# Adding seven expert groups' rows through a DRAM table, and expert weights in long runs, in a two-layer attention and mixture-of-experts kernel

## The chip, the cores and the metric

The kernel runs on one core of a Trainium2 chip. The metric is device time in microseconds (us), lower is better. Times shown are the median of three runs and, for the trace, one profiled execution.

## What is computed

Four sequences of 256 tokens with 256 features (1024 tokens) go through two layers. The change touches only the end of the second one, the expert part:

```python
probs = jax.nn.softmax(x @ Wr, axis=-1)                       # 32 experts
topw, topi = jax.lax.top_k(probs, K)                          # K = 4 per token
topw = topw / jnp.sum(topw, axis=-1, keepdims=True)
shared = silu(x @ Wsg) * (x @ Wsu) @ Wsd                      # shared expert
shared = shared * jax.nn.sigmoid(x @ Wse)
xe = jnp.zeros((E, CAP, h), x.dtype).at[sel, posc].add(x[tok] * valid[:, None])   # CAP = 32 slots
g = silu(jnp.einsum('ech,ehf->ecf', xe, Wg))
u = jnp.einsum('ech,ehf->ecf', xe, Wu)
ye = jnp.einsum('ecf,efh->ech', g * u, Wd)
y_pair = ye[sel, posc] * (w * valid)[:, None]
out = shared.at[tok].add(y_pair)
```

Beside it stands the second attention, whose values are weighed, transposed and multiplied by a projection. The output is the first layer's x plus that projection, the shared expert and the experts' weighted rows.

## The kernel before

Bass code with a block for each engine; each block is a list of instructions in a fixed order, tied to the others by semaphores. Arrays of tokens are eight tiles of 128 tokens by 256 features.

**Experts.** 32 experts times 32 slots are 1024 slots, handled as `GR` = 8 groups of 128 slots (four experts each). For each group GpSimd (POOL) gathers the rows of its tokens from the DRAM table `token_rows` (line 624), and the list `EXPERT_STEPS` (lines 33 to 43) sets the order in which every engine takes its part. For TensorE (PE): "slots" transposes the gathered rows, "up" (line 1317) multiplies by Wg and Wu, "turn" transposes the hidden rows, "down" (line 1337) multiplies by Wd into bank 7, "sd" (lines 1350 and 1352) is a tile of the shared expert's second product. In the first four tiles of "sd" both operands are plain float32; in the others, and in the projection, each operand is split into a rounded high and a low part, and `mm3` (lines 945 to 947) adds three products.

**Mixing.** After "down" VectorE (DVE) copies a group's output to `YE` (line 1889), ScalarE (ACT) writes its weighted high part `YH` (line 891), DVE the low part `YL` (line 1859). DVE also builds for each group a mask `GT[g]` of 128 slots by 1024 tokens (line 1855). For every one of the eight token tiles PE then multiplies each group's mask by `YH` and by `YL` (lines 1361 and 1362: 2 x 8 x 8 = 128 products) and adds the projection's six into the same bank. "mix" steps bring the first six groups of four tiles forward into the list; the rest comes behind it.

**Second attention's values.** POOL multiplies probabilities by values and adds them (lines 634 and 638, 32 instructions for eight tiles), PE transposes the result (line 1400), ACT and DVE split it, `mix_proj` multiplies.

**Loads.** SyncE (SP) issues nearly all DMAs (lines 482 to 508): for each group two of Wg and Wu (704 KB each, runs of 176 floats) and two of Wd, into four places that are used twice. Groups 4 to 7 wait until the place is free.

**End.** DVE adds each finished bank into `X` (line 1870), SP stores the tile (line 511).

Of the kernel before, what the change touches and what calls it, by code (L numbers as in the profile page):

```python
# [34 lines left out]
                 ("turn", 0), ("slots", 3), ("up", 2), ("down", 0), ("turn", 1), ("slots", 4), ("up", 3), ("down", 1), ("turn", 2), ("sd", 1),  # L35
                 ("mask", (4, 5)), ("split", 0), ("weigh", 0), ("down", 2), ("turn", 3), ("split", 1), ("split", 2), ("sd", 2),
                 ("split", 3), ("down", 3),
                 ("up", 4), ("slots", 5), ("split", 4), ("sd", 3), ("split", 5), ("turn", 4), ("split", 6), ("up", 5), ("slots", 6),
                 ("mask", (6,)), ("down", 4), ("mask", (0,)), ("sd", 4), ("mask", (1, 2)), ("turn", 5),
                 ("mask", (3,)), ("sd", 5), ("mask", (7,)), ("down", 5),  # L40
                 ("high", 0), ("up", 6), ("slots", 7), ("high", 3), ("low", 0), ("sd", 6), ("turn", 6), ("low", 3),
                 ("sd", 7), ("add", 7), ("down", 6), ("mix", 0), ("mix", 1), ("up", 7), ("mix", 2), ("turn", 7),
                 ("mix", 3), ("down", 7)]
# [14 lines left out]
TC = 2 * E1 + 1  # L58
EPS = 1e-5
MASKED = -1.0e30  # L60


def program(nc, a, out):
    ctx = ExitStack()
    with ctx:
# [113 lines left out]
        WD = [w.rearrange("p (e c n) -> p e c n", e=EPG, c=2)  # L179
# [3 lines left out]
        def up_weights(g, e):  # L183
# [5 lines left out]
        GT = [nc.alloc_sbuf_tensor_at(f"GT{g}", [P, N], FR, offset=at)  # L189
              for g, at in enumerate([at0 + 4 * N * k for k in range(4)] + [at0 + 4 * (28672 + N * k) for k in range(2)]  # L190
                                     + [at_xt + 4 * (5 * C * N // 2), at1 + 4 * 2944])]
        YH = nc.alloc_sbuf_tensor_at("YH", [P, GR, D], FR, offset=at0 + 4 * GR * N)
        YL = OS[:, 1].rearrange("p s h n -> p (s h n)").rearrange("p (g n) -> p g n", g=GR)
        TK = IT = FRF[:, 2944:2944 + N]
        HTE = region(15872, 512).rearrange("p (i k n) -> p i k n", i=2, k=2)
# [50 lines left out]
        s_x = [sem(f"x_loaded{b}") for b in range(B)]  # L246
# [1710 lines left out]
```

## Time and profile before

| | |
|---|---|
| median of 3 runs | 428.7 us (428.68 to 429.19) |
| the profiled execution's own time | 429.21 us |
| its span in the trace | 426.8 us |
| granted TensorE clock | 1.0 of full speed |
| PE, PEld busy | 98%, 88% |
| DVE, ACT, POOL busy | 73%, 58%, 40% |
| DMA traffic | 34.45 MB, mean 81 GB/s |

The span is the time from the first to the last recorded event; the execution's own time is 2.4 us longer. PE is the multiplying part of TensorE, PEld its loading of weights, which runs beside it. A matmul's recorded duration contains its way through the array, so that neighbours overlap: what one costs in a row of many is the distance from start to start. A plain float32 product is recorded as two instructions. Times in the trace count from the start of the span.

### The profile page before, as it was taken

The numbers are of one execution on the slowest core, as the hardware profiler recorded it, in microseconds if no ns is written. First come the engines' busy times: TensorE is split into PE (matmuls) and PEld (weight loads), VectorE is DVE, ScalarE is ACT, GpSimd is POOL, SyncE is SP. The second block draws the span as 40 slices with busy tenths as digits, with TensorE's granted clock in tenths as the row PEclk, the third lists the DMA queues.
The fourth block names the chain that finished last, engine by engine and source line by source line (L and its number), as shares of the span: only waits on it lengthen the run. The fifth ranks groups of instructions, "written<-read, shape, count | busy, mean of one in ns | idle before, by whom it ended". The sixth has DMA issues, their size and how long they took to land.

```text
span 426.8 us, 8853 instructions
## 1 busy us (share of the span) xinstructions
PE 419.8 (98%) x3070; PEld 377.2 (88%) x3070; DVE 310.9 (73%) x910; ACT 247.5 (58%) x671; POOL 168.6 (40%) x293
## 2 busy tenths in 40 slices
PE   8999999999999999999999999999999999999997
PEld 8788879999999999999999999999997777567797
DVE  5967575787787888787877767657689994688442
ACT  4666741887868788777867786434314622563120
POOL 3520002645554554554554530102077007699200
DMA  7800020501010101010000000000099942899002
GB/s 214 303 2 1 2 76 25 198 1 51 2 51 0 51 2 51 2 52 1 2 0 3 2 2 0 27 14 12 26 321 300 307 115 88 236 305 279 9 14 86
DMA packets 37754, 34.45 MB, mean 81 GB/s; under 512 B 2448, under 2 KB 35920, under 8 KB 37712
## 3 DMA queue, kind: packets, MB, share of 16 engines
q1 hardware_dynamic: 37328, 32.85, 26.2%
q0 software_dynamic: 384, 1.05, 0.8%
q8 instruction: 25, 0.41, 0.4%
q14 instruction: 17, 0.14, 0.1%
HBM read 31.80 MB, written 2.10 MB: 79 GB/s over the span
## 4 chain that ended last, share of the span: by engine, by line
PE 92%; DVE 5%; ACT 2%; issue 1%; POOL 0%; POOLq 0%; DVEq 0%
PE bank L945 21%; PE bank L947 21%; PE bank L946 21%; PE bank L1116 5%; PE bank L1128 3%; PE bank L1107 3%; PE bank L1350 2%; PE bank L1317 2%; PE bank L1361 2%; PE bank L1362 2%; PE bank L1158 2%; PE bank L1337 2%; DVE OS L1859 1%; PE bank L1022 1%; PE bank L1266 1%; DVE arena L1499 1%
## 5 line engine op out<-in xcount | busy, mean ns | idle before, releaser
L587 POOL TENSOR_TENSOR arena<-arena,rinv 128x384 f32<-128x384 f32 x64 | 52.9, 828 | 81.0 <-DVE rinv L1629 81.0
L945 PE MATMUL bank<-XTl,WA 128*128 128x512 f32 (+1 forms) x126 | 52.0, 412 | 0.9 <-DVE arena L1499 0.8
L947 PE MATMUL bank<-XTh,WA 128*128 128x512 f32 (+1 forms) x126 | 49.1, 390 | 0.0
L946 PE MATMUL bank<-XTh,WA 128*128 128x512 f32 (+1 forms) x126 | 49.1, 389 | 0.0
L771 ACT ACTIVATE PT<-bank 128x256 fp32r<-128x256 f32 x64 | 24.5, 383 | 34.0 <-PE bank L1116 34.0
L1633 DVE TENSOR_TENSOR PT<-bank,PT 128x256 fp32r<-128x256 f32 x64 | 27.2, 425 | 18.8 <-ACT arena L772 18.8
L945 PE MATMUL bank<-WA,XTh 128*128 128x256 f32 x128 | 38.3, 299 | 0.0
L578 POOL CAST Q<-arena 128x128 fp32r<-128x128 f32 x64 | 18.7, 292 | 47.0 <-PE bank L947 47.0
L946 PE MATMUL bank<-WA,XTl 128*128 128x256 f32 x128 | 35.7, 279 | 0.0
L947 PE MATMUL bank<-WA,XTh 128*128 128x256 f32 x128 | 35.7, 279 | 0.0
L1621 DVE CUSTOM_DVE_ANT_0 arena<-bank,posm 128x128 f32<-128x128 f32 x64 | 18.1, 283 | 20.8 <-PE bank L947 20.8
L764 ACT ACTIVATE arena<-arena,nmax 128x256 f32<-128x256 f32 x64 | 32.3, 505 | 0.0
L580 POOL TENSOR_TENSOR Q<-arena,Q 128x128 fp32r<-128x128 f32 x64 | 29.6, 463 | 5.1
L1116 PE MATMUL bank<-ident,arena 128*128 128x128 f32 x192 | 31.4, 272 | 0.0
L777 ACT ACTIVATE arena<-bank,VC 128x256 f32<-128x256 f32 x64 | 30.1, 470 | 0.1
L945 PEld LDWEIGHTS bank<-XTl,WA 128*128 128x128 f32 x126 | 23.8, 189 | 5.5 <-issue 1.7
L947 PEld LDWEIGHTS bank<-XTh,WA 128*128 128x128 f32 x126 | 23.7, 188 | 5.3
L680 ACT ACTIVATE arena<-bank,bqs 128x512 f32<-128x512 f32 x16 | 18.4, 1148 | 15.6 <-PE bank L947 14.7
L946 PEld LDWEIGHTS bank<-XTh,WA 128*128 128x128 f32 x126 | 23.8, 189 | 3.8
L1623 DVE CUSTOM_DVE_ANT_0 arena<-bank,posm 128x256 f32<-128x256 f32 x64 | 26.8, 419 | 0.0
L762 ACT ACTIVATE arena<-arena,nmax 128x128 f32<-128x128 f32 x64 | 25.9, 404 | 1.6 <-DVE nmax L1623 1.1
L749 ACT ACTIVATE K<-bank,VC 128x512 fp32r<-128x512 f32 x32 | 22.0, 688 | 7.5 <-PE bank L947 7.5
(329 smaller groups left out, 1455.5 us busy)
## 6 DMA issues: line engine op xcount, KB each, us to landing
arena<-in_L_ffn_Wg SPq DMA_DIRECT2D x6, 704.0 KB, 7.8
arena<-in_L_ffn_Wu SPq DMA_DIRECT2D x6, 704.0 KB, 10.3
arena<-in_L_ffn_Wd SPq DMA_DIRECT2D x6, 512.0 KB, 7.2
arena<-in_L_attn_Wk SPq DMA_DIRECT2D x8, 256.0 KB, 2.6
arena<-in_L_attn_Wv SPq DMA_DIRECT2D x8, 256.0 KB, 3.2
arena<-in_L_attn_Wo SPq DMA_DIRECT2D x1, 2048.0 KB, 8.4
arena<-in_L_ffn_Wd SPq DMA_DIRECT2D x6, 192.0 KB, 7.6
arena<-in_L_attn_Wq SPq DMA_DIRECT2D x4, 256.0 KB, 4.7
```

The lines of the kernel that those rows point to most:

```text
L580: pool.tensor_tensor(QL[:, u % 3], q, QH[:, u % 3].bitcast(F32), ALU.subtract).then_inc(s_qh, 1)
L587: pool.tensor_tensor(pr, pr, r[:, :, None].to_broadcast([P, 3, P]), ALU.mult).then_inc(s_p, 1)
L762: nc.scalar.activation(Pb[i][:, 0:128], Pb[i][:, 0:128], ACT.Exp, bias=nmax[:, i, 0:1], scale=-1.0, accum_out=psumr[:, i, 0:1])
L764: nc.scalar.activation(Pb[i][:, 128:384], Pb[i][:, 128:384], ACT.Exp, bias=nmax[:, i, 1:2], scale=-1.0, accum_out=psumr[:, i, 1:2]).then_i ...
L771: nc.scalar.activation(PTH[:, u % 2], pb[2 + u % 2][:, 0:256], ACT.Copy)
L777: nc.scalar.activation(QO[:, h, b], pb[4 + u % 2][:, 0:256], ACT.Identity, bias=VC[:, 32 + h:33 + h]).then_inc(s_Oc, 1)
L945: pe.matmul(dst, wh, xl, start=start, stop=False)
L946: pe.matmul(dst, wl, xh, start=False, stop=False)
L947: return pe.matmul(dst, wh, xh, start=False, stop=stop)
L1116: ins = pe.transpose(pb[2 + u % 2][:, P * i:P * i + P], Pb[u % 3][:, P * i:P * i + P], ident[:])
L1623: nc.vector.tensor_tensor_reduce(Pb[i][:, 128:384], bank[:, 128:384], MASK, -1.0, -MASKED, ALU.add, ALU.min, nmax[:, i, 1:2]).then_inc(s_m, 1)
L1633: nc.vector.tensor_tensor(PTL[:, u % 2], pb[2 + u % 2][:, 0:256], PTH[:, u % 2].bitcast(F32), ALU.subtract).then_inc(s_Tl, 1)
```

## The change

**Experts' rows.** Groups 0 to 6 no longer go through masks. ACT writes a group's weighted output, in float32, to `YW` (`y_weighted`). PE multiplies it by a 128 x 128 matrix `SAME[:, g]`, which is 1 where two slots of the group belong to one token ("merge", `expert_merge`), so that each of those slots holds the sum for its token. ACT copies the sum to `YZ` (`y_merged`), and POOL adds the 128 rows into a DRAM table `expert_rows` by an indirect DMA that accumulates (`scatter`), one behind the other: each waits until the one before has landed. Slots whose token came earlier in the group are sent to a spare row. SP fills the table with zeros near the start of the kernel, and at the end, after the seventh scatter has landed, loads it back in four DMAs of 256 KB; DVE adds it to `X` (`add_rows`). Group 7 still uses a mask, one pair of products for each tile.

**What this needs.** Two products of one row by 512 columns (in `table_turn`) spread the slots' token numbers; DVE compares them (`same_token`), POOL clears the part above the diagonal (`BEFORE`), DVE forms the list of rows (`row_places`).

**Order.** `EXPERT_STEPS` has "merge", "ranks", "values" and "ao" steps in place of "high", "low", "mix" and most "mask" steps. "ao" brings the transposes of the values forward. The last tile's values move from POOL to DVE (`last_values`, 7 instructions), POOL follows the list `PV_STEPS`. "sd" alternates between two banks in place of three.

**Weights.** numpy lays out Wg and Wu side by side and ordered by partition, Wd likewise; a group's "up" weights are one DMA (two where its place has two parts) with 11264 bytes in a run for each partition, and Wd's runs are 4096 bytes.

```diff
-                 ("sd", 7), ("add", 7), ("down", 6), ("mix", 0), ("mix", 1), ("up", 7), ("mix", 2), ("turn", 7),
-                 ("mix", 3), ("down", 7)]
...
+                 ("down", 5), ("values", 0), ("turn", 6), ("sd", 5), ("merge", 5), ("down", 6), ("up", 7), ("values", 1), ("merge", 6), ("sd", 6),
+                 ("turn", 7), ("ao", 0), ("down", 7), ("ao", 1), ("sd", 7), ("add", 7)]
...
+LAST = GR - 1
...
+FINAL_BANK = (1, 4, 5, 6, 0, 2, 7, 3)
+PV_STEPS = [("values", 0, 0, 1), ("values", 1, 0, 1), ("values", 2, 0, 2), ("scatter", 0), ("values", 3, 0, 2), ("scatter", 1),
+            ("values", 4, 0, 3), ("scatter", 2), ("values", 5, 0, 3), ("scatter", 3), ("values", 6, 0, 2), ("scatter", 4),
+            ("values", 6, 2, 4), ("scatter", 5), ("scatter", 6)]
...
-            return (0, 2, 3)[j % 3]
+            return (0, 2)[j % 2]
...
+            sp.dma_start(expert_rows.rearrange("(g p) d -> p g d", p=P), ZR[:, None, :].to_broadcast([P, GR + 1, D])).then_inc(s_xs, 16)
...
+                m = EPG // len(WGU[i])
+                for h, part in enumerate(up_parts[i]):
+                    sp.dma_start(part, a["experts_up"][g, :, m * h:m * h + m].rearrange("p e c n -> p (e c n)")).then_inc(s_ew[i], 16)
...
+            sp.wait_ge(s_xg[LAST - 1], 32)
+            for k in range(B):
+                sp.dma_start(YS[:, 2 * k:2 * k + 2], expert_rows[2 * P * k:2 * P * k + 2 * P].rearrange("(g p) d -> p g d", p=P)).then_inc(s_x[k], 16)
...
+            pool.wait_ge(s_gt, 2)
+            pool.affine_select(out=BEFORE, in_=SAME[:, 0:LAST], compare_op=ALU.is_gt, fill=0.0, base=0,
+                               pattern=[[0, LAST], [-1, P]], channel_multiplier=1).then_inc(s_it, 1)
+            pool.iota(IT, [[1, N]], base=1, channel_multiplier=0, allow_small_or_imprecise_dtypes=True).then_inc(s_it, 1)
...
+            def scatter(g):
+                if g == 0:
+                    pool.wait_ge(s_rk, 1)
+                else:
+                    pool.wait_ge(s_xg[g - 1], 32)
+                pool.wait_ge(s_yr, g + 1)
+                pool.indirect_dma_start(expert_rows, bass.IndirectOffsetOnAxis(ap=rank[:, g:g + 1], axis=0), YZ[:, g % 2], None,
+                                        compute_op=ALU.add).then_inc(s_xg[g], 16)
...
+            def y_weighted(g):
+                act.wait_ge(s_dn, g + 1)
+                act.wait_ge(s_sw1, 1)
+                if g == LAST:
+                    nc.scalar.activation(YH[:], pb[7][:, 0:D], ACT.Copy, scale=slot_w[:, g:g + 1]).then_inc(s_ye, 1)
+                    return
+                if g >= 2:
+                    act.wait_ge(s_mg, g - 1)
+                nc.scalar.activation(YW[:, g % 2], pb[7][:, 0:D], ACT.Copy, scale=slot_w[:, g:g + 1]).then_inc(s_ye, 1)
+
+            def y_merged(g):
+                act.wait_ge(s_mg, g + 1)
+                if g >= 2:
+                    act.wait_ge(s_xg[g - 2], 32)
+                nc.scalar.activation(YZ[:, g % 2], pb[3][:, 0:D], ACT.Copy).then_inc(s_yr, 1)
...
+                for half in range(2):
+                    ins = pe.matmul(pb[4 + half][:], onesr[0:1, :], TKr[0:1, 512 * half:512 * half + 512], start=True, stop=True)
+                    ins.then_inc(s_tt, 1)
...
+            def expert_merge(g):
+                pe.wait_ge(s_ye, g + 1)
+                if g >= 1:
+                    pe.wait_ge(s_yr, g)
+                pe.matmul(pb[3][:, 0:D], SAME[:, g], YW[:, g % 2], start=True, stop=True).then_inc(s_mg, 1)
...
-            def mix_groups(j, groups, start, stop):
-                dst, ts = mix_tile(j)
-                for g in groups:
-                    pe.matmul(dst, GT[g][:, ts], YH[:, g], start=start and g == groups[0], stop=False)
-                    ins = pe.matmul(dst, GT[g][:, ts], YL[:, g], start=False, stop=stop and g == groups[-1])
-                return ins
...
+            def values_turn(half):
+                if half == 0:
                     pe.wait_ge(s_xe, GR)
-                    pe.wait_ge(s_gt, GR)
-                    pe.wait_ge(s_yl, 6)
-                mix_groups(j, range(6), True, False)
+                    pe.wait_ge(s_eh, GR - 1)
+                    pe.wait_ge(s_pv, 8)
+                else:
+                    pe.wait_ge(s_eh, GR)
+                    pe.wait_ge(s_ec, GR)
+                    pe.wait_ge(s_pv, 25)
+                    pe.wait_ge(s_pd, 1)
+                for c in range(C):
+                    for i in range(4):
+                        ins = pe.transpose(pb[ao_bank(c, half)][:, P * i:P * i + P], AO[:, 4 * half + i, P * c:P * c + P], ident[:])
+                    ins.then_inc(s_at, 1)
...
+            def final_tile(j):
+                dst, ts = pb[FINAL_BANK[j]][:, 0:D], slice(P * j, P * j + P)
                 for c in range(C):
-                    ins = mm3(dst, AOTh[:, c, ts], AOTl[:, c, ts], PJh[:, c], PJl[:, c], False, c == C - 1)
-                ins.then_inc(s_fo, 1)
-
-            for j in range(4):
-                mix_groups(j, range(6, GR), False, False)
-            for j in range(4, NT):
-                pe.wait_ge(s_al, j - 3)
-                mix_groups(j, range(GR), True, False)
+                    mm3(dst, AOTh[:, c, ts], AOTl[:, c, ts], PJh[:, c], PJl[:, c], c == 0, False)
+                pe.matmul(dst, GT[:, ts], YH[:], start=False, stop=False)
+                pe.matmul(dst, GT[:, ts], YL[:], start=False, stop=True).then_inc(s_fo, 1)
+
+            pe.wait_ge(s_pjl, 1)
+            pe.wait_ge(s_al, 4)
+            pe.wait_ge(s_gt, 3)
+            pe.wait_ge(s_ye, GR + 1)
+            for j in range(NT):
                 if j == 4:
-                    pe.wait_ge(s_al, 4)
-                    pe.wait_ge(s_pjl, 1)
-                mix_proj(j - 4)
-            for j in range(4, NT):
-                mix_proj(j)
+                    pe.wait_ge(s_x2, NT - 1)
+                if j == 5:
+                    pe.wait_ge(s_x2, NT)
+                if j == NT - 1:
+                    pe.wait_ge(s_yr, LAST)
+                final_tile(j)
...
+            def same_token(half):
+                n = 4 if half == 0 else LAST - 4
+                dve.wait_ge(s_tt, 2 + half)
+                nc.vector.scalar_tensor_tensor(out=SAME[:, 4 * half:4 * half + n], in0=pb[4 + half][:, 0:P * n].rearrange("p (g n) -> p g n", g=n),
+                                               scalar=1.0, in1=slot_t[:, 4 * half:4 * half + n, None].to_broadcast([P, n, P]),
+                                               op0=ALU.max, op1=ALU.is_equal).then_inc(s_gt, 1)
+
+            def row_places():
+                dve.wait_ge(s_it, 4)
+                nc.vector.tensor_reduce(earlier[:], BEFORE, AX, ALU.add)
+                step(nc.vector.tensor_scalar(slot_d[:], slot_t[:, 0:LAST], spare[:, 0:1], None, ALU.subtract))
+                step(nc.vector.scalar_tensor_tensor(out=slot_d[:], in0=earlier[:], scalar=0.0, in1=slot_d[:], op0=ALU.is_gt, op1=ALU.mult))
+                nc.vector.scalar_tensor_tensor(out=rank[:], in0=slot_t[:, 0:LAST], scalar=-1.0, in1=slot_d[:],
+                                               op0=ALU.add, op1=ALU.subtract).then_inc(s_rk, 1)
+
+            def last_values(part):
+                j = NT - 1
+                for k in (0, 1) if part == 0 else (2, 3):
+                    dst = AO[:, j] if k == 0 else pvt2
+                    p, v = value_operands(j, k)
+                    step(nc.vector.tensor_tensor(dst.rearrange("p (g r d) -> p g r d", g=G1, r=4), p, v, ALU.mult))
+                    if k:
+                        ins = nc.vector.tensor_tensor(AO[:, j], AO[:, j], pvt2, ALU.add)
+                        if k == 3:
+                            ins.then_inc(s_pd, 1)
+                        else:
+                            step(ins)
+
+            def last_low():
+                dve.wait_ge(s_ye, GR)
+                nc.vector.scalar_tensor_tensor(out=YL[:], in0=pb[7][:, 0:D], scalar=slot_w[:, LAST:GR], in1=YH[:].bitcast(F32),
+                                               op0=ALU.mult, op1=ALU.subtract).then_inc(s_ye, 1)
+
+            def add_rows(j):
+                dve.wait_ge(s_x[j // 2], 32)
+                step(nc.vector.tensor_tensor(X[:, j], YS[:, j], X[:, j], ALU.add))
...
+    up = np.concatenate([given['L1_ffn_Wg'], given['L1_ffn_Wu']], axis=2)
+    out['experts_up'] = up.reshape(GR, EPG, C, P, 2 * F1).transpose(0, 3, 1, 2, 4)
+    out['experts_down'] = given['L1_ffn_Wd'].reshape(GR, EPG, F1, D).transpose(0, 2, 1, 3).reshape(GR, F1, EPG * D)
```

The last part of the PE program, before: down of group 7 (L1337), all transposes of the values (L1400), then masks times `YH` and `YL` (in `OS`); 56 more such pairs and the 48 products of the projection follow or stand between.

```order
L1337 MATMUL bank<-WAF,arena 32x256 x8
L1400 MATMUL bank<-ident,arena 128x128 x16
L1361 MATMUL bank<-YH,GT_73 128x256
L1362 MATMUL bank<-OS,GT_73 128x256
L1361 MATMUL bank<-YH,GT_74 128x256
L1362 MATMUL bank<-OS,GT_74 128x256
```

Now (rows of three kinds: L1397 is down, L1377 up, L1405 merge, L1387 and L1388 turn, L1433 transposes of the values; between the merge and the turn stand the 18 products of sd 6, before the last rows the 18 of sd 7):

```order
L1397 MATMUL bank<-arena 32x256 x8
L1377 MATMUL bank<-arena 32x352 x8
L1405 MATMUL bank<-YX,arena 128x256
...
L1387 MATMUL bank<-ident,arena 128x128
L1388 MATMUL bank<-ident,arena 48x128
L1433 MATMUL bank<-ident,arena 128x128 x8
L1397 MATMUL bank<-WAF,arena 32x256 x8
L1433 MATMUL bank<-ident,arena 128x128 x8
...
L1464 MATMUL bank<-Y_69,GT 128x256
L1465 MATMUL bank<-Y_70,GT 128x256
```

A tile's end is now the projection's six products and one pair for group 7; the sums of groups 0 to 6 have left the PE program but for one merge each.

POOL behind the gathers, before (L634 multiplies, L638 adds; the end of its program):

```order
L634 TENSOR_TENSOR pvt<-arena 128x256
L638 TENSOR_TENSOR arena<-arena,pvt 128x256
L634 TENSOR_TENSOR pvt<-arena 128x256
L638 TENSOR_TENSOR arena<-arena,pvt 128x256
L65 UNCONDITIONAL_BRANCH
```

And now (L665 and L669 are the same two, L679 a scatter):

```order
L679 DMA expert_rows<-YX_68,rank 1152x256
L665 TENSOR_TENSOR pvt<-arena 128x256
L669 TENSOR_TENSOR arena<-arena,pvt 128x256
L665 TENSOR_TENSOR pvt<-arena 128x256
L669 TENSOR_TENSOR arena<-arena,pvt 128x256
L679 DMA expert_rows<-YX_68,rank 1152x256 x2
L68 UNCONDITIONAL_BRANCH
```

The scatters stand among the values; between the fifth and the sixth are four value instructions, between the sixth and the seventh none.

## Rows read from the trace of the kernel before

**Rows 1.** The chain that ended last, by engine (the page).
```profile
PE 92%; DVE 5%; ACT 2%; issue 1%; POOL 0%; POOLq 0%; DVEq 0%
```
**Rows 2.** Stretches: us, busy time (and instructions) of each engine, clock, DMA share, GB/s.
```profile
365.00:385.00 20.00, 20.00 (x198) 12.23 (x196) 15.72 (x28) 12.14 (x29) 16.93 (x19) 1.00 1.13 298
385.00:398.00 13.00, 13.00 (x134) 10.56 (x126) 11.85 (x20) 3.96 (x12) 11.31 (x14) 1.00 0.84 211
398.00:407.00 9.00, 8.60 (x86) 6.89 (x82) 1.06 (x4) 1.26 (x4) 0.00 (x0) 1.00 0.01 2
407.00:427.00 20.00, 17.15 (x148) 16.85 (x144) 7.78 (x16) 2.98 (x6) 0.00 (x0) 1.00 0.15 53
```
**Rows 3.** PE's waits from 350 us: us in total, times, longest.
```profile
PE bank L1361 <- DVE X L1864: 0.4, 1, 0.4
```
**Rows 4.** PE groups by line from 350 us: count | busy us, mean ns | idle before.
```profile
L1361 PE MATMUL bank<-YH,GT 128*128 128x256 f32 x64 | 15.9, 288 | 0.4 <-DVE X L1864 0.4
L1362 PE MATMUL bank<-OS,GT 128*128 128x256 f32 x64 | 15.5, 281 | 0.0
```
**Rows 5.** PE and DVE in order of time: start, us, what.
```profile
340.82 0.63 PE L1266 MATMUL bank<-FRX,TW 128*65 128x512 f32 x2
341.29 0.40 PE L945 MATMUL bank<-XTl,OS 128*128 128x512 f32 x1
...
370.60 1.46 PE L1350 MATMUL bank<-FRF,arena 128*128 128x256 f32 x6
371.90 1.03 PE L1350 MATMUL bank<-FRF,WAF 128*128 128x256 f32 x4
372.76 0.59 PE L1350 MATMUL bank<-FRF,arena 128*128 128x256 f32 x2
373.29 1.07 PE L1337 MATMUL bank<-arena 128*32 128x256 f32 x16
...
410.07 0.28 PE L1361 MATMUL bank<-YH,GT 128*128 128x256 f32 x1
...
411.01 0.28 PE L1361 MATMUL bank<-YH,GT 128*128 128x256 f32 x1
...
424.26 0.42 DVE L1870 TENSOR_TENSOR X<-bank,X 128x256 f32<-128x256 f32 x1 [0.28 <-PE bank L947]
```
**Rows 6.** ACT groups by line from 350 us.
```profile
L891 ACT ACTIVATE YH<-arena,slot_w 128x256 fp32r<-128x256 f32 x8 | 3.6, 502 | 8.6 <-DVE arena L1889 5.8 <-PE bank L1337 2.7
L903 ACT ACTIVATE arena<-bank 128x256 f32<-128x256 f32 x8 | 3.0, 380 | 0.1
```
**Rows 7.** POOL in order of time.
```profile
353.92 0.95 POOL L624 DMA_INDIRECT arena<-token_rows,idx  x1 [0.30 <-issue]
...
366.66 2.09 POOL L634 TENSOR_TENSOR arena<-arena 128x256 f32<-128x256 f32 x3 [3.27 <-DVE arena L1793]
...
391.74 0.65 POOL L634 TENSOR_TENSOR arena<-arena 128x256 f32<-128x256 f32 x1
```
**Rows 8.** DMA issues: count, KB each, us from issue to landing.
```profile
arena<-in_L_attn_Wk SPq DMA_DIRECT2D x8, 256.0 KB, 2.6
arena<-token_rows,idx POOLq DMA_INDIRECT x8, 2.8
out<-X SPq DMA_DIRECT2D x8, 128.0 KB, 1.7
arena<-in_L_ffn_Wu SPq DMA_DIRECT2D x3, 704.0 KB, 10.1
```
**Rows 9.** The stores of `token_rows`, from issue to landing.
```profile
DMA to landing us min/median/max: 1.7/1.7/8.0
```
**Rows 10.** SP's last issue of Wu, and PE's first product that reads it.
```profile
383.88 2.01 SPq L495 DMA_DIRECT2D arena<-in_L_ffn_Wu  x1
...
401.50 1.39 PE L1317 MATMUL bank<-arena 128*32 128x352 f32 x16
```
**Rows 11.** DVE groups by line from 350 us.
```profile
L1855 DVE TENSOR_SCALAR GT<-FRF,slot_t 128x1024 fp32r<-128x1024 f32 x8 | 7.7, 991 | 0.0
L1859 DVE SCALAR_TENSOR_TENSOR OS<-arena,slot_w,YH 128x256 fp32r<-128x256 f32 x8 | 5.4, 708 | 0.2 <-ACT YH L891 0.2
L1870 DVE TENSOR_TENSOR X<-bank,X 128x256 f32<-128x256 f32 x8 | 3.4, 425 | 9.4 <-PE bank L947 9.4
L1889 DVE COPY arena<-bank 128x256 f32<-128x256 f32 x8 | 3.3, 418 | 4.0 <-PE bank L1337 3.9
```

More of the change, by code:

```diff
@@ L243, in program @@
         pvt = sb("pvt", [P, 256])
-        s_x = [sem(f"x_loaded{b}") for b in range(B)]
+        onesr = sb("onesr", [1, P], FR)
+        spare = sb("spare", [P, 1])
+        earlier = sb("earlier", [P, LAST])
+        slot_d = sb("slot_d", [P, LAST])
+        rank = sb("rank", [P, LAST], U32)
+        expert_rows = nc.dram_tensor("expert_rows", (N + P, D), F32, kind="Internal").ap()
+        s_x = [sem(f"x_then_expert_rows_loaded{b}") for b in range(B)]
         s_xb0 = sem("x_second_tile_loaded")
@@ L629, in _, with values @@
+            pool.iota(IT, [[1, N]], base=1, channel_multiplier=0, allow_small_or_imprecise_dtypes=True).then_inc(s_it, 1)
+            chain = [0]
+            def values(j, k0, k1):
                 pool.wait_ge(s_ap, 1 + j // 6)
[L630 to L632 removed]
+                for k in range(k0, k1):
+                    p, v = value_operands(j, k)
@@ new lines, in scatter @@
+            def scatter(g):
[6 more added lines that the diff above has]
+                                        compute_op=ALU.add).then_inc(s_xg[g], 16)
+            for what, *n in PV_STEPS:
+                if what == "values":
+                    values(*n)
+                if what == "scatter":
+                    scatter(*n)
@@ L1874, in _ @@
                     shared_product(n[0])
+                if what == "shared" and n == (11, 1):
+                    same_token(0)
+                    same_token(1)
                 if what == "table":
@@ L1886, in _ @@
                     nc.vector.tensor_tensor(HE[:, n % 2], HE[:, n % 2], pb[4 + n % 2][:, F1:2 * F1], ALU.mult).then_inc(s_eh, 1)
-                if what == "down":
-                    dve.wait_ge(s_dn, n + 1)
-                    nc.vector.tensor_copy(YE[:, n], pb[7][:, 0:D]).then_inc(s_ye, 1)
+                if what == "down" and n == LAST:
+                    last_low()
+                if what == "ranks":
+                    row_places()
+                if what == "values":
+                    last_values(n)
+                if what == "ao":
+                    if n == 0:
+                        dve.wait_ge(s_pjh, 1)
+                        nc.vector.tensor_tensor(PJl[:], projT[:], PJh[:].bitcast(F32), ALU.subtract).then_inc(s_pjl, 1)
+                    for c in range(C):
+                        xs = slice(512 * n, 512 * n + 512)
+                        dve.wait_ge(s_ac, 2 * n + c + 1)
+                        nc.vector.tensor_tensor(AOTl[:, c, xs], pb[ao_bank(c, n)][:], AOTh[:, c, xs].bitcast(F32), ALU.subtract).then_inc(s_al, 1)
                 if what == "up" and n == 0:
@@ L1900, in _ @@
                 if what == "mask":
-                    for g in n:
-                        dve.wait_ge(s_it, 4)
-                        slot_mask(g)
-                if what == "low":
-                    for g in range(n, n + 3):
-                        y_low(g)
+                    dve.wait_ge(s_it, 5)
+                    nc.vector.tensor_scalar(GT[:], IT, slot_t[:, LAST:GR], None, ALU.is_equal).then_inc(s_gt, 1)
                 if what == "sd" and n >= 1:
@@ L1910, in _ @@
                     add_shared(n)
[L1911 to L1918 removed]
+            for j in range(NT):
+                add_rows(j)
             for j in range(NT):
```

173 lines of the change are left out of this document (72 added, 101 removed).

## The prediction

> **What bounds the kernel now.** I read first the chain that ended last: 92% of it is PE [rows 1]. Then the stretches: from 365 us to the end PE is busy throughout but for 0.4 us at 398 and the last 3 us [rows 2], and from 350 us on that 0.4 us is the only wait that PE has on anyone [rows 3]. Granted clock 1.00 in every stretch: PE runs at 2.4 GHz, and no stretch says that this changes. So in the last 75 us the time is the number of PE's products times their distance, and a product that goes shortens the kernel as long as nothing else ends later. Next, the groups by line: 128 products mix the experts' rows into the tokens [rows 4]. The last one that counts is DVE's last addition at 424.26 [rows 5]; behind it are 0.42 us, a store of 1.7 us [rows 8] and the end at 426.8. That is the profiled execution's span; its own time is 429.21, and the median of the runs 428.7, 0.5 us lower. I work out a difference from the trace and take it from the median.
>
> **PE's work, term by term.**
> - Removed: 128 mixing products become 16 (one pair for each tile), 112 fewer. Their mean of 281 to 288 ns is not the cost, since neighbours overlap; eight lie between 410.07 and 411.01 [rows 5], 0.118 us each. 112 x 0.118 = 13.2 us, all on the path.
> - Added: seven merges, plain float32, 128 x 256. The twelve records of L1350 from 370.60 to 373.29 [rows 5] are six such products: 2.69 / 6 = 0.45 us each, 3.1 us in all.
> - Added: two products of 512 columns on one row. L1266 has two of 512 columns between 340.82 and 341.29 [rows 5]: 0.47 us. (One row instead of 128 contracts less, but as many columns pass.)
> - Moved, not changed: the 16 transposes of the values, the "up" and "down" steps, the projection's 48 products.
> - Sum: -13.2 + 3.1 + 0.5 = -9.6 us.
>
> **Do new waits take this back?** PE's order has a cross-engine step in front of each merge: ACT writes the weighted rows (0.50 us, L891 [rows 6]) and later copies the sum out of bank 3 (0.38 us, as L903). In the order list at least a "down" or a "sd" or an "up" (1 to 2.7 us of PE) stands between a "down" and its merge or between a merge and the next. Only at the third group is ACT late by about as much as PE takes: it has behind sd 1 a copy, the split of SD, a table load and an exponential. I walked through the list with these durations and found PE waiting there by 0.1 to 0.3 us, and the present 0.4 us at 398 gone: nothing in total. In the middle ACT has 12.1 of 20 us busy [rows 2], and 7 x 0.38 = 2.7 us of work are new to it (the weighing was there already). DVE gets lighter: seven masks of 0.99 us, seven low parts of 0.71 and eight copies of 0.42 [rows 11] go, 15.2 us; the last tile's values, two comparisons, the list of rows and eight additions of 0.42 come. The two banks of "sd" ask of DVE only that it is one tile behind; it does these additions at the step before.
>
> **The layout of the weights: 0.** No row has PE waiting for a weight [rows 3]. The last Wu is issued at 383.9 and lands after about 10.1 us [rows 8, 10], 394; PE reads it at 401.5 now, and at about 397.3 in the new order, where up 7 has fewer products before it. Three us are left even with the old layout. The engines are full from 365 to about 396 at 298 GB/s [rows 2]; longer runs can only end that sooner, and free the queues for the scatters. If it were worth nothing at all, the sum would stand. The Trainium skill (DMA: Bandwidth & Descriptors, Rules for kernel authors) says to coalesce small transfers and use at least 1 MiB per DMA for bandwidth; by it the new "up" loads (1408 KB in one piece) are quicker, but here a quicker load would shorten nothing. The zeros at the start (1.2 MB) go out behind the first weights, and what follows them in the queue is issued at 54 us; 0 as well.
>
> **The second chain: POOL, scatters, loading back.** This is new and can end later than PE. POOL starts on the values at 366.66 and begins the last tile at 391.74 [rows 7], so the 25 instructions that it keeps take 25.1 us. New start 0.5 later, 367.2. Five scatters before the sixth, at the price of a gather's issue, 0.95 + 0.30 [rows 7]: 6.3 us. The list of rows is late for the first one, about 1 us. Sixth scatter at 367.2 + 25.1 + 6.3 + 1 = 399.6. Landing: a gather of the same 128 rows takes 2.8 us [rows 8], so 402.4; the seventh, which waits for it, lands at 405.2. (Its merge ends at about 399.7 on PE, so it is not waited for.) SP then loads: 2.6 us for a first piece of 256 KB [rows 8], three more at 300 GB/s 2.6 us, 410.4. DVE adds the last two tiles (0.85) and then the eight banks (about 0.39 apart): the last addition could start at 411.3 + 2.7 = 414.0. PE's chain puts it at 424.26 - 9.6 = 414.7. So PE ends last, with 0.7 us to spare.
>
> **The unknown price** is the accumulating scatter; no row shows one. Lower bound: the gather, 2.8 us; nothing excludes slightly less, but less gains nothing, since PE then ends last. Upper bound in quiet: it reads the rows and then stores, 2.8 + 1.7 [rows 8] = 4.5 us. Two landings stand in series, so the upper bound moves the second chain by 3.4 us, 2.7 beyond PE. Its issue costs POOL between 0.95 and, with a second list of descriptors, 1.9 us: up to 7 x 0.95 = 6.7 more. Against this stands that POOL's value instructions are stretched by DVE (0.65 us alone at 391.74, 1.0 on the average), and DVE loses 15 us of work. I take 2.8 and 1.25, nearest to the gather, which has the same rows, engine and queue. The Trainium skill (DMA: Bandwidth & Descriptors, Latency and other measured facts) puts an access to HBM at 0.2 us on average and 2 us at high load. By it the first scatters, which run beside the weights, land up to 1.8 us later; behind each stand three to five value instructions (3 to 5 us) before the next needs it, so the sum would be the same, and the last two run after the weights.
>
> **Forecast:** 428.7 - 9.6 = 419.1 us.
>
> **The rivals.**
> - *The scatter chain ends last.* For: 0.7 us of slack is less than either unknown. Against: POOL's stretched instructions give back. With both upper bounds it is 6.7 + 3.4 - 0.7 = 9.4 later at the worst, with half of each 4.4: 423.5. Chance 0.25 for 420.6 to 426.
> - *ACT becomes the pacer of the middle.* If every copy of a sum (0.38) and its weighing (0.50), which DVE did not have in PE's turn before, appears on PE: 7 x 0.88 = 6.2 us, 425.3; a third of it, 421.1. Against: the steps between. Chance 0.07.
> - *Slower: scatters beside the weights crawl.* The stores of `token_rows` land in 1.7 us, but one took 8.0 behind loads [rows 9]. The scatters are strictly in series. The last loading must begin 415.6 or later for the span to reach 426.8 (5.2 of loading, 0.85 and 3.1 on DVE, 2.1 behind). From the first at about 373, seven in a row reach that at (415.6 - 373) / 7 = 6.1 us each. At 8.0 they reach 429, and the kernel takes 428.7 + 13.3 = 442. Against: from 396 the engines are quiet [rows 2], so the last two or three cannot all take this. Chance 0.07.
> - *The change does not shorten PE:* the products go but PE waits for POOL's 25 values at the second "ao" (at about 403, POOL done at 399.6). From 3.5 us of POOL lateness on PE stops; this comes with the first rival, with the same price. Chance 0.01 of no change.
>
> **How the numbers follow.** PE ends last or within 1.5 us of it: 0.60, 417.6 to 420.6 (the distances per product are good to a few per cent, 0.5 us; small waits up to 1 us either way). The range reaches through the first rival to 425.0, and from below starts at 417.6; outside lie the slower case and tails, 0.12 or so. A measurement of this kernel can tell a difference of 0.2% (0.9 us) from none. Faster by more than 0.2%: 0.60 + 0.25 + 0.07 less tails = 0.91; same 0.02; slower 0.07.
>
> **What would show it.** Right: L1464 and L1465 have 8 products each at 0.118 us distance; merges 0.45 each; the last DVE addition 9 to 10 us earlier, released by PE; SP's wait for the last scatter ends before 406; POOL's scatters near 1 us, landing near 3. The first rival: the last additions of DVE are back to back, released by the loads, and PE done before. The second: PE waits for ACT before L1405 or L1397. The slower case: landings over 6 us while the weights load. It would be wrong at its root if PE's products in the new end stood further apart than 0.118 us.

## The result and the profile after

The changed kernel takes 435.3 us (median; 433.69 to 435.95), the kernel before, in the same comparison, 428.9 (428.68 to 429.69): ratio 1.0136, 95% interval 1.011 to 1.0161. It is slower by 6 us where 9.6 us less had been forecast.

| | before | after |
|---|---|---|
| the profiled execution's own time, its span | 429.21, 426.8 us | 435.95, 433.9 us |
| granted TensorE clock | 1.0 | 0.984 |
| PE busy, matmuls | 419.8 us, 3070 | 413.5 us, 2974 |

The chain that ended last (the page of the kernel after; of before: [rows 1]). PE's share fell from 92% to 85%, and DMA, which had none, has 6%:

```profile
PE 85%; DMA 6%; DVE 3%; issue 3%; ACT 2%; SPq 0%; POOL 0%; DVEq 0%; POOLq 0%; ACTq 0%
```

The waits from 350 us on, of the kernel after: us in total, times, longest. Where PE had one wait of 0.4 us [rows 3], it has two that matter, and both are on ACT:

```profile
POOL expert_rows L679 <- issue: 11.3, 2, 6.1
ACT YX L949 <- DMA expert_rows<-YX,rank: 9.7, 2, 7.5
...
DVE X L1948 <- DMA arena<-expert_rows: 6.2, 2, 3.9
PE bank L1397 <- ACT arena L972: 5.9, 1, 5.9
...
PE bank L1405 <- ACT YX L943: 1.6, 1, 1.6
```

ACT in turn waits for a scatter. L949 is `y_merged`: its copy of group 2's sum into `YZ` needs the buffer that group 0's scatter still reads, since there are two. The same kernel in order of time, the seven scatters on POOL first, then the two waits of ACT and the two of PE (in brackets: idle before, and what ended it):

```profile
373.26 1.65 POOL L679 DMA_INDIRECT expert_rows<-YX,rank  x1 [2.64 <-DVE rank L1925]
383.25 1.59 POOL L679 DMA_INDIRECT expert_rows<-YX,rank  x1 [6.12 <-issue]
393.87 1.59 POOL L679 DMA_INDIRECT expert_rows<-YX,rank  x1 [5.20 <-issue]
400.78 1.60 POOL L679 DMA_INDIRECT expert_rows<-YX,rank  x1 [0.46 <-POOL arena L669]
405.42 1.60 POOL L679 DMA_INDIRECT expert_rows<-YX,rank  x1 [0.75 <-POOL arena L669]
410.51 1.74 POOL L679 DMA_INDIRECT expert_rows<-YX,rank  x1 [0.46 <-ACT YX L949]
415.07 1.57 POOL L679 DMA_INDIRECT expert_rows<-YX,rank  x1 [2.83 <-DMA expert_rows<-YX,rank]
...
382.58 0.38 ACT L949 ACTIVATE YX<-bank 128x256 f32<-128x256 f32 x1 [2.24 <-DMA expert_rows<-YX,rank]
393.23 0.38 ACT L949 ACTIVATE YX<-bank 128x256 f32<-128x256 f32 x1 [7.47 <-DMA expert_rows<-YX,rank]
...
383.90 0.70 PE L1405 MATMUL bank<-YX,arena 128*128 128x256 f32 x2 [1.61 <-ACT YX L943]
395.02 1.94 PE L1397 MATMUL bank<-arena 128*32 128x256 f32 x16 [5.92 <-ACT arena L972]
```

Scatter 0 is issued at 373.26 and ACT, which waits for it, moves on at 382.58: it landed after 9.3 us. Scatter 1 landed at 393.1, after 9.9. The waits on "issue" before the second and third scatter are the same landings, which the profile did not tie to a DMA. The third scatter is already in quiet: the DMA share is 0.00 from 394 to 396, and its 144 packets pass between 396.0 and 397.3, the last of them 3.5 us after its issue. From it on the gaps between scatters are 4.6 to 6.9 us, and POOL's own values fill all but the last. The stretches of the kernel after show what PE's stop at 389 brings with it (columns as in [rows 2]; the clock is the third number from the end):

```profile
384.00:389.00 5.00, 5.00 (x34) 3.34 (x34) 1.39 (x5) 1.74 (x3) 4.36 (x6) 1.00 1.03 325
389.00:395.00 6.00, 0.10 (x1) 0.00 (x0) 0.84 (x2) 1.77 (x6) 1.13 (x2) 0.83 0.62 194
395.00:397.20 2.20, 1.94 (x16) 0.59 (x16) 2.20 (x4) 1.13 (x4) 2.12 (x3) 0.50 0.54 59
397.20:399.70 2.50, 2.42 (x11) 2.45 (x12) 1.80 (x3) 0.29 (x1) 2.27 (x4) 0.50 0.01 1
399.70:403.00 3.30, 3.30 (x31) 1.93 (x29) 0.00 (x0) 0.93 (x4) 2.84 (x3) 1.00 0.05 2
```

PE idles for 5.9 us, and when it starts again the granted clock is 0.50, that is 1.2 GHz, until 399.7; then it is 2.4 GHz again. The sixteen products of "down" take 1.94 us at 395.02 (1.07 at 373.29 in [rows 5]) and the next ones stand about 0.21 us apart (0.118 later on): 0.9 + 11 x 0.09 = 1.9 us on top of the 7.5 of waiting (and 0.3 more, in which PE waits for VectorE at 397.28).

The end, from the chain of the kernel after: start, us, what.

```profile
410.51 3.97 DMA expert_rows<-YX,rank
414.48 0.59 issue
415.07 3.80 DMA expert_rows<-YX,rank
418.89 0.38 SPq L534
419.31 0.47 SPq L534
419.83 5.83 DMA arena<-expert_rows
425.75 0.44 DVE X L1948
```

and VectorE's last instructions:

```profile
421.65 1.80 DVE L1948 TENSOR_TENSOR X<-arena,X 128x256 f32<-128x256 f32 x4 [3.92 <-DMA arena<-expert_rows]
425.75 1.80 DVE L1948 TENSOR_TENSOR X<-arena,X 128x256 f32<-128x256 f32 x4 [2.30 <-DMA arena<-expert_rows]
427.58 2.74 DVE L1958 TENSOR_TENSOR X<-bank,X 128x256 f32<-128x256 f32 x8
```

PE's last product starts at 424.5 (423.88 before); VectorE's last addition starts at 429.9 and ends at 430.3. Two things ended later than forecast, then: PE by 10 us, and the second chain (scatters, loading back, additions) by 16. The two are tied: the sixth scatter, at 410.51, waited for ACT's copy of its sum (idle "0.46 <-ACT YX L949" above), and so for PE, though POOL's values would have held it until 410.05 in any case.

### The profile page after: what moved, and what is told of

Read it like the earlier page. It is cut to its first block, busy times and chain, and to the rows that moved or that the text cites. A ratio compares the mean times of both kernels' runs of the same rounds, so it can differ in the third digit from the quotient of the medians.

```text
span 433.9 us, 8696 instructions
## 1 busy us (share of the span) xinstructions
PE 413.5 (95%) x2974; PEld 368.1 (85%) x2974; DVE 305.6 (70%) x909; ACT 249.4 (57%) x678; POOL 171.7 (40%) x297
## 4 chain that ended last, share of the span: by engine, by line
PE 85%; DMA 6%; DVE 3%; issue 3%; ACT 2%; SPq 0%; POOL 0%; DVEq 0%; POOLq 0%; ACTq 0%
PE bank L1000 21%; PE bank L1002 21%; PE bank L1001 20%; DMA expert_rows<-YX,rank 5%; PE bank L1171 5%; PE bank L1183 3%; PE bank L1162 3%; PE bank L1377 2%; PE bank L1213 2%; DMA arena<-expert_rows 1%; PE bank L1077 1%; PE bank L1321 1%; PE bank L1039 1%; PE bank L1397 1%; PE bank L1416 1%
## 6 DMA issues: line engine op xcount, KB each, us to landing
FRF<-in_experts_up SPq DMA_DIRECT2D x2, 704.0 KB, 10.4
```

## The experiments

My theory after the two traces: the scatters that run beside the weights land late; as each waits for the one before, and ACT for the one before the last, this moves both PE and the end. Rivals: the long runs of weights do it, ACT's wait alone does it, or the scatter is dear in itself. The experiments ran in four sets; "before" is the kernel before in the same set. Times of the kernels are medians of 4 to 10 executions. Ratios are compared across sets.

| kernel | median us (lowest to highest) | before | ratio [95%] |
|---|---|---|---|
| the changed kernel | 435.3 (433.7 to 436.0) | 428.9 | 1.0136 [1.011, 1.0161] |
| layout_only | 428.8 (427.5 to 429.2) | 428.2 | 1.0002 [0.9988, 1.0015] |
| old_layout | 432.6 (432.5 to 433.0) | 428.2 | 1.0100 [1.0075, 1.0125] |
| middle_runs | 431.9 (430.3 to 433.0) | 428.2 | 1.0081 [1.0054, 1.0109] |
| four_places | 433.0 (432.2 to 433.2) | 428.2 | 1.0099 [1.0073, 1.0126] |
| no_add | 426.6 (426.1 to 428.5) | 429.6 | 0.9943 [0.9925, 0.9961] |
| no_reload | 427.0 (426.0 to 428.0) | 429.6 | 0.9947 [0.9931, 0.9964] |
| two_tables | 424.5 (424.0 to 425.8) | 429.6 | 0.9892 [0.9873, 0.9911] |
| two_tables_middle | 424.8 (424.1 to 425.7) | 429.6 | 0.9894 [0.9874, 0.9914] |
| order_only | 433.3 (432.1 to 434.1) | 428.3 | 1.0112 [1.0087, 1.0137] |
| two_tables_long | 425.6 (424.8 to 426.6) | 428.3 | 0.9939 [0.9917, 0.9962] |
| two_tables_order | 422.0 (420.9 to 422.5) | 428.3 | 0.9858 [0.9841, 0.9874] |
| two_tables_order_long | 422.0 (421.3 to 422.3) | 428.3 | 0.9849 [0.983, 0.9868] |

**The new layout alone**, in the kernel before.

```diff
-                for k, n in enumerate(("Wg", "Wu")):
-                    w = a["L1_ffn_" + n][e].rearrange("e (c p) n -> p e c n", p=P)
...
-                        sp.dma_start(part[:, :, :, F1 * k:F1 * k + F1], w[:, m * h:m * h + m]).then_inc(s_ew[i], 16)
+                for h, part in enumerate(up_parts[i]):
+                    sp.dma_start(part, a["experts_up"][g, :, m * h:m * h + m].rearrange("p e c n -> p (e c n)")).then_inc(s_ew[i], 16)
```

> The kernel before with the weights' new layout alone. Theory A (long runs hold up the scatters, and nothing else in the kernel reads beside the weights): 428.9 us within 0.3%, PE waits on no weight in either kernel. Rival B (the layout hurts by itself, or helps by itself): off by over 1 us. The weights of groups 4 to 7 should be in by about 387 instead of 396.

Measured: 1.0002, no difference, and PE still has no wait on a weight. The last load was issued at 379.0 instead of 389.4, and the last weights are in at 393.4 instead of 396.1 (387 had been expected). The layout by itself costs and gives nothing in time.

**The old layout in the changed kernel** (the diff above, reversed).

> The changed kernel with the old layout of the weights (704-byte and 1024-byte runs), scatters as they are. Theory A: the second scatter lands in 5 us or less instead of 9.9, ACT's waits on scatters (9.7 us) shrink to under 2, PE's stalls at 382 and 389 (7.5 us) go, and the time is 421 to 425. Rival C (an accumulating scatter is slow beside any stream of loads that fills the engines): landing stays at 8 us or more and the time within 2 us of 435.3.

Measured: 1.0100, 432.6 us: theory A, with 421 to 425, missed, and rival C is nearer. PE's waits on ACT are 0.3 and 2.9 us instead of 1.6 and 5.9. The scatters, on POOL:

```profile
372.79 1.65 POOL L681 DMA_INDIRECT expert_rows<-YX,rank  x1 [3.14 <-DVE rank L1927]
381.48 1.59 POOL L681 DMA_INDIRECT expert_rows<-YX,rank  x1 [4.83 <-issue]
389.04 1.59 POOL L681 DMA_INDIRECT expert_rows<-YX,rank  x1 [2.15 <-issue]
398.21 1.60 POOL L681 DMA_INDIRECT expert_rows<-YX,rank  x1 [2.74 <-issue]
```

The distances are 8.7, 7.6 and 9.2 us here; 10.0, 10.6 and 6.9 with the long runs. The short runs make the first two scatters less late, but they also go on longer, the last packet of the weights ending at 397.4 instead of 394.1, so that the third scatter is late as well (it lands after 8.4 us). The fourth is issued 2.6 us earlier than in the changed kernel.

**Runs of 1408 bytes**, between the 704 of before and the 11264 of the change (Wd as before).

```diff
-                for h, part in enumerate(up_parts[i]):
-                    sp.dma_start(part, a["experts_up"][g, :, m * h:m * h + m].rearrange("p e c n -> p (e c n)")).then_inc(s_ew[i], 16)
+                for h, part in enumerate(WGU[i]):
+                    sp.dma_start(part, a["experts_up"][g, m * h:m * h + m].rearrange("e c p n -> p e c n")).then_inc(s_ew[i], 16)
```

> The changed kernel with up weights in runs of 1408 bytes in DRAM (Wg and Wu side by side, not ordered by partition) and Wd in its old 1024-byte runs. Theory A: landing of the scatters beside the loads between the two, nearer to the old layout since the run is 8 times shorter than 11264: time 422 to 427. Rival C: as the changed kernel, 435. If it is not the run but the number of DMAs issued that counts, it is as the changed kernel too.

Measured: 1.0081, 431.9 us, a miss too (422 to 427 had been expected); distances 8.8 and 8.7 us. With runs twice as long the time is no worse than with the old ones, and with runs of 11264 bytes it is 1.5 us (by ratios) to 2.6 us (by medians) more than the old layout. The intervals of those two just overlap; the traces show the fourth scatter 2.6 us later. So the long runs are a part of the loss, 1 to 3 us of it, and not its base. In the 10 us from 373 the changed kernel's weights come in 589 packets of 5.6 KB on the average, the old layout's in 3842 of 0.7 KB. The Trainium skill (DMA: Bandwidth & Descriptors, Queues, rings and completion order) says that a DMA engine alternates between the queues that have work, a packet at a time. By that rule a scatter's packet waits longer behind longer ones. The traces agree in direction: the 144 packets of the first two scatters are spread over 3.5 and 3.6 us with the long runs (378.3 to 381.8, 389.0 to 392.7), over 2.1 and 2.0 with the old ones, and over 1.3 in quiet. That is not the whole: with either layout 4.3 to 5.8 us pass from a scatter's issue to its first packet beside the weights, 2.3 in quiet (410.51 to 412.83), and no run shows what they go into.

**Four buffers for the merged rows** instead of two, so that ACT waits for the scatter four before.

```diff
+        YZ = [YX[:, 2], YX[:, 3], region(22016, D), region(22016 + D, D)]
...
-                if g >= 2:
-                    act.wait_ge(s_xg[g - 2], 32)
+                if g >= 4:
+                    act.wait_ge(s_xg[g - 4], 32)
```

> The changed kernel with four instead of two buffers for the merged rows, so that ACT's copy of group g waits for scatter g-4. Theory A (PE stalls because ACT stands in front of a scatter): ACT's 9.7 us of waits and PE's 7.5 us of stalls with the half clock behind them go, and PE's products end near 414. But POOL's own series of scatters is as long as before, so the end comes from the last scatter and the loading back: 430 to 434 us. Rival D (only ACT's wait counts): 423 or less.

Measured: 1.0099, 433.0 us, within theory A's 430 to 434; rival D, with 423 or less, is out. But PE's products do not end near 414: its two stops are gone, and a third has come, the only wait of PE from 350 on:

```profile
409.22 1.94 PE L1434 MATMUL bank<-ident,arena 128*128 128x128 f32 x8 [5.71 <-POOL arena L670]
```

L1434 is the second "ao": it waits for POOL's values. POOL takes its list in order; while a scatter waits for the landing of the one before (11.2 us in all in this trace), the values behind it wait too. ACT's wait was one way from the scatters to PE, and behind it lay the next. The seventh scatter is issued at 413.78 instead of 415.07.

**Scatters that store instead of adding**, so that the sums are left out.

```diff
-                                        compute_op=ALU.add).then_inc(s_xg[g], 16)
+                ... YZ[:, g % 2], None).then_inc(s_xg[g], 16)
```

> The changed kernel with each of the seven scatters storing its rows instead of adding them (a token's row in the table is then the last group's part alone: the addition is left out). If the addition in memory is what makes a scatter take 3.8 us in quiet and 7 to 10 us beside the weights, the landings fall to the row loads' own 1.7 to 2.8 us, and the time falls by 5 us or more, to about 430. If the price is that of a small indirect transfer behind other traffic, whatever it does at its end, landings and time stay within 1 us of the changed kernel's.

Measured: 0.9943, 8 us below the changed kernel. Neither reading holds whole: the time fell as the first has it, and so did most landings in quiet; those beside the weights did not. POOL, of no_add:

```profile
374.06 1.04 POOL L679 DMA_INDIRECT expert_rows<-YX,rank  x1 [2.50 <-DVE rank L1924]
381.74 1.12 POOL L679 DMA_INDIRECT expert_rows<-YX,rank  x1 [4.42 <-issue]
```

and three landings from its chain, one beside the weights, two in quiet:

```profile
381.74 7.81 DMA expert_rows<-YX,rank
...
405.85 4.19 DMA expert_rows<-YX,rank
...
410.62 2.40 DMA expert_rows<-YX,rank
```

In quiet the last plain scatter lands after 2.4 us, an adding one after 3.8; on POOL it takes 1.0 us and an adding one 1.6. The addition's price is thus about 1.4 us of landing and 0.6 of POOL. The 1.4 is less sure: the plain scatter before the last took 4.2 us with no load beside it (its packets are spread over 2.1 us, those of the other three in quiet over 0.5), which stays open. The nine times fall into two groups, 426.1 to 426.6 and 428.3 to 428.5, and the profiled execution is of the second. But beside the weights the plain one still needs 7.8 us (9.9 with the addition): most of the lateness there is not the addition's. A plain scatter is 48 packets, an adding one 144. At the end of the chain the seventh scatter has landed at 413.0 instead of 418.9, and the last rows are back at 418.0 instead of 425.7, which is the 8 us.

**No weights loaded for groups 4 to 7**, so that the scatters run in quiet; these groups compute with the weights of groups 0 to 3.

```diff
-            for g in range(GR):
+            for g in range(PLACES):
```

> The changed kernel with the weight loads of groups 4 to 7 left out (those groups compute with the weights of groups 0 to 3), so that no load runs beside the scatters. If the weights' traffic is what makes the first three scatters late, all seven land in 3.7 to 4.1 us, ACT's waits on a scatter (9.7 us in the changed kernel) and PE's two stalls (7.5 us) go, and the time falls by about 7 us, to 428: the last scatter is then bound by POOL's own values. If the lateness belongs to the scatters themselves (cold code, the chain of seven on one engine), it stays at 433 or more.

Measured: 0.9947; PE has no stop. The end of its chain:

```profile
401.50 4.03 DMA expert_rows<-YX,rank
...
406.13 3.85 DMA expert_rows<-YX,rank
409.99 3.56 DMA arena<-expert_rows
```

The seventh scatter lands at 409.98 instead of 418.89. Of the changed kernel's loss 8.9 us of this chain are thus the weights beside the scatters. The rest stays: even in quiet this design is only 0.5% faster than before.

**Two tables.** The theory now says: take the serial waits out and the lateness of a scatter costs nothing. Even and odd groups add into a table of their own, a scatter waits for the one before the last, there are four buffers, the layout is the old one, and the odd table is loaded back and added while the last scatter is still under way.

```diff
-                else:
-                    pool.wait_ge(s_xg[g - 1], 32)
+                if g >= 2:
+                    pool.wait_ge(s_xg[g - 2], 32)
...
-                pool.indirect_dma_start(expert_rows, bass.IndirectOffsetOnAxis(ap=rank[:, g:g + 1], axis=0), YZ[:, g % 2], None,
+                pool.indirect_dma_start(expert_rows[g % 2], bass.IndirectOffsetOnAxis(ap=rank[:, g:g + 1], axis=0), YZ[g % 4], None,
...
+            for i, dst, ready in ((1, YS1, s_wq), (0, YS, s_x)):
+                sp.wait_ge(s_xg[LAST - 1 - i], 32)
```

> The changed kernel with the layout of before, four buffers for merged rows, and even and odd groups scattered into two tables, so that a scatter waits only for the one before the last; the odd groups' table is loaded back and added to X before the last scatter has landed. If the serial chain of seven is the bound, the last scatter leaves about 5 us earlier, and with half of the additions done early the time is 421 to 425, below both kernels. If POOL's own time is the bound (its values and 1.6 us per scatter), the last scatter leaves 2 us earlier at most, and the time stays at 429 to 432.

> As two_tables, with the weights in 1408-byte runs in place of 704. If only the chain counts, equal to it within 1 us. If longer runs delay the scatters even when two may be in flight, slower by 1 us or more.

Measured: 0.9892 and 0.9894, faster than before and equal to each other. No wait on a landing is left on POOL or ACT, though landings stay late (the one that the trace of two_tables_middle shows took 7.7 us), and the last scatter is issued 12 us earlier than in the changed kernel. PE's last products, of two_tables:

```profile
413.40 0.28 PE L1470 MATMUL bank<-Y,GT 128*128 128x256 f32 x1
413.51 0.28 PE L1471 MATMUL bank<-Y,GT 128*128 128x256 f32 x1
```

and the engines' busy time:

```profile
PE 410.0 (97%) x2974; PEld 365.4 (87%) x2974; DVE 310.3 (73%) x917; ACT 249.5 (59%) x678; POOL 173.6 (41%) x297
```

PE is busy 9.8 us less than before (419.8), and its last product starts at 413.51 (423.88 before; 414.3 by the forecast). The time fell by less, about 5 us, since VectorE's additions of rows and products now end last, at 418.9. This set changes several things at once; what of its 2.4% is the tables', the buffers' or the earlier odd additions was not taken apart.

> two_tables with the changed kernel's long runs of weights. If the long runs cost time only through the chain (a scatter that waits for the one before it, an activation that waits for a scatter), they cost nothing here either, as in two_tables_middle: 424 to 425. If a scatter is now late by so much that even the wait for the one before the last counts, it is 426 or more.

Measured: 0.9939, a miss: 0.5% above two_tables. Its first scatter is issued at 374.27 and the seventh at 404.58, those of two_tables at 372.59 and 403.0: all later by 1.6 to 1.7 us, and none by more. PE's busy time in the first 100 us is 96.1 us against 96.9. So the difference lay ahead of the scatters, which says nothing yet on whether the layout causes it; hence the last run below.

**The order of the last additions.** In the changed kernel VectorE waits for the rows and then adds the products, each of which had long been ready.

```diff
-            for j in range(NT):
-                add_rows(j)
-            for j in range(NT):
-                add_rest(j)
+            for j in range(NT):
+                add_rest(j, False)
+            for j in range(NT):
+                add_rows(j, True)
```

> The changed kernel with VectorE's last sixteen additions in another order: the eight products are added while the table's rows are still on their way, the rows last, and no addition waits for the one before it on another tile. If the time after the last landing counts in full, the 5.5 us from the first late rows to the last addition shrink to about 3 us, and the time falls by 2 to 2.6 us, to about 433. If TensorE, which finishes its last product at 424.7, were the end, nothing would change.

Measured: 1.0112, 1.0 us less by ratios and 2.0 by medians; the intervals of the two kernels overlap, so by the times alone it could be nothing. The trace shows the step itself:

```profile
424.42 0.42 DVE L1951 TENSOR_TENSOR X<-bank,X 128x256 f32<-128x256 f32 x1 [0.51 <-PE bank L1465]
424.77 2.76 DVE L1951 TENSOR_TENSOR X<-arena,X 128x256 f32<-128x256 f32 x8
```

The products are added as PE delivers them, the eight row additions follow in 2.76 us, and the last one ends at 427.5 instead of 430.3. Of these 2.8 us 0.8 are not the order's: in this trace the seventh scatter was issued at 414.26, in the changed kernel's at 415.07.

> two_tables with the same change of order (products of tiles 0 and 1, the odd table's rows, products 2 to 4, the even table's rows, products 5 to 7). Here TensorE ends at 413.9 and the even table's rows come at 412.5, so that eight row additions of 0.34 and three products of 0.34 remain: the last addition ends at about 416.3 in place of 418.9, and the time is about 422. If the stores that follow it wait for something else, it stays at 424.5.

Measured: 0.9858, 422.0 us, as expected. The end, of two_tables_order:

```profile
411.80 1.08 DVE L1957 TENSOR_TENSOR X<-bank,X 128x256 f32<-128x256 f32 x3
412.79 2.76 DVE L1957 TENSOR_TENSOR X<-arena,X 128x256 f32<-128x256 f32 x8
415.47 1.08 DVE L1957 TENSOR_TENSOR X<-bank,X 128x256 f32<-128x256 f32 x3
```

> two_tables_order with the long runs of weights. two_tables_long came out 0.5% above two_tables, but its first scatter was already 1.6 us late when it was issued, and every later one by the same 1.6: from the first scatter on the long runs cost it nothing. If those 1.6 us are a difference from one kernel to another in the first 20 us of the program, they need not come again, and the ratio is 0.984 to 0.988 as for two_tables_order (0.9858). If they belong to the layout, it is 0.990 or more here too.

Measured: 0.9849. The first scatter is issued at 372.94, and the long runs cost nothing here. The 1.6 us did not come again and were not the layout's. Either version of two_tables_order is the fastest kernel of this study, 1.4 to 1.5% below the kernel before.

## Why the prediction was wrong

- **PE's work, -9.6: right.** Where no scatter holds PE up, its busy time falls from 419.8 to 410.0 us and its last product starts 10.4 us earlier (two_tables); 0.4 of that is the old wait. The merges (two records, 0.4 us) and the pair per tile are as costed.
- **"Do new waits take this back? ... nothing in total": wrong, the first failed step.** I costed the steps between engines with their durations alone. `y_merged` also waits for the scatter two before, which stands in the quoted code, and I never put a landing in there. PE stood 7.5 us, and the 1.2 GHz behind it cost 1.9 more.
- **"The first scatters, which run beside the weights, land up to 1.8 us later; behind each stand three to five value instructions ... so the sum would be the same": wrong, the step that turns the sign.** The landings were 9.3 and 9.9 us, 5.4 to 6 above the quiet 3.9, and three to five value instructions do not cover that. Without the weights beside them (no_reload) the kernel is at 0.9947 instead of 1.0136. The Trainium skill (DMA: Bandwidth & Descriptors, Latency and other measured facts) has 2 us for an access to HBM at high load, against 0.2 on the average; the measured addition is three times that difference, and the measurement decides. My own rows had the warning: one store of `token_rows` took 8.0 us behind loads [rows 9].
- **The layout, 0: right alone, wrong in company.** I wrote that longer runs "can only ... free the queues for the scatters". They ended sooner (394.1 instead of 397.4) and made the scatters later while they ran: 1 to 3 us in the chain of seven, nothing once that chain is loosened.
- **The price of a scatter: between the bounds, but I took the lower end.** Landing in quiet 3.8 to 4.0 us (2.8 taken, 4.5 the upper bound), POOL 1.6 + 0.3 to 0.46 (1.25 taken, up to 2.2 allowed). In no_reload, where only this counts, the sixth is issued at 401.5 (399.6 forecast) and the seventh lands at 410.0 (405.2): 4.8 us.
- **The end.** The last addition starts at 429.9 instead of 414.0, 15.9 us: 8.9 from the weights beside the scatters (418.89 less 409.98), 4.8 from the price of a scatter, 1.6 from loading back (6.8 us from landing to the last rows, 5.2 forecast), 1.0 from the additions behind it, four of them at 0.46 where I had counted two; 0.4 go off again, since the eight last ones are closer together than the 0.39 that I took.
- **The rivals.** "Scatters beside the weights crawl" was the case that came, with a chance of 0.07. Its point of decision was right: from 6.1 us each in series the kernel is slower; the seven took (418.89 - 373.26) / 7 = 6.5. Against it I had put that the last ones run in quiet. They did, and so did the third; but two landings of 9.3 and 9.9 us and POOL's own work between the others (4.6 to 6.9 us from one to the next) are enough. "PE waits for POOL's 25 values at the second ao" came too, 5.7 us, as soon as ACT's wait was taken away. The sign that I had given for "ACT becomes the pacer", PE waiting for ACT before L1405 and L1397, is in the trace as well, but for another reason: ACT stood before a landing, and its own work grew by 1.9 us (249.4 busy, 247.5 before) where 2.7 had been forecast.

## What to carry to other kernels

Before small transfers are put in series beside a large stream of loads, give each the landing that such a transfer has beside that stream (the longest in the trace, not the median), and then ask of every engine in the cycle, the issuing one first, what it holds up while it waits for a landing. Two tables and enough buffers made landings as late as these harmless, and PE's work then ended as its sum had promised; of the 9.6 us the time gained about 5, and 6 with the new order of additions. Which of the two, tables or buffers, does how much was not tested. Work that is ready goes ahead of the work that waits for the last transfer.

## What the runs showed of the hardware

- An accumulating scatter of 128 rows of 1 KB lands in quiet after 3.8 to 4.0 us, a plain one after 2.4 and once after 4.2 (no_add); on POOL they take 1.6 and 1.0 us, a gather 0.95. The adding one has three times the packets (144 and 48).
- Beside loads that fill the DMA engines (share 1.0) the landings are 9.3 and 9.9 us with runs of 11264 bytes, and 7.6 to 9.2 us pass from one scatter to the next with runs of 704.
- After PE had idled for 5.9 us the clock was 1.2 GHz until 399.7; after the stop of 1.6 us at 382 it stayed at 2.4 GHz. In old_layout, after a stop of 2.9 us that ended at 390.2, the granted clock is 0.50 in the stretch from 393 to 397, 1.2 GHz as well.
